# A first batch of 256 tokens taken tile by tile in a fused attention and FFN layer

## The reference

```
xn  = layernorm(x)
s   = attention(xn)            # Wqkv, 16 heads of 16, softmax(q k^T / 4) v, Wproj, bproj
g   = silu(gelu(xn W1^T + b1) W2^T + b2)      # 1024 hidden features
out = x + s * g
```

## Time and profile before

| | |
|---|---|
| time, three runs | 120.67, 120.86, 120.93 us |
| the profiled execution | 120.73 us |
| its span in the trace | 118.9 us |
| PE (TensorE) busy | 113.7 us (96% of the span) |
| VectorE, ScalarE, GpSimd busy | 84.8, 74.3, 70.3 us |
| TensorE at work without a break | from 7.63 us to 115.4 us |
| last store issued | 116.76 us |

### The profile page before, as it was taken

The page is one execution under the profiler, slowest core; times in us unless marked ns, Lnnn a source line. Parts: engine busy times, 40 slices in busy tenths (PEclk is TensorE's granted clock), DMA queues, the critical chain, the costliest instruction groups (busy, mean ns, idle before and its releaser), DMA issues.

```text
span 118.9 us, 2560 instructions
## 1 busy us (share of the span) xinstructions
PE 113.7 (96%) x930; PEld 88.4 (74%) x930; DVE 84.8 (71%) x159; ACT 74.3 (62%) x109; POOL 70.3 (59%) x91
## 2 busy tenths in 40 slices
PE   6989999999999999999999999999999999999980
PEld 5589998887878987888768777776775867566660
DVE  0799994520997989999899498205955848998762
ACT  4063795469979302231295979899868888799000
POOL 4227678009999904877889759589614341517460
PEclk9999999999999999999999999999999999999999
DMA  2999932666565366520000004500000000020213
GB/s 107 298 366 375 330 88 68 205 201 205 203 207 205 121 207 206 199 90 6 7 13 3 0 0 145 215 8 8 11 0 0 0 6 0 13 75 9 85 58 121
DMA packets 9632, 13.27 MB, mean 112 GB/s; under 512 B 2452, under 2 KB 4884, under 8 KB 9492
## 3 DMA queue, kind: packets, MB, share of 16 engines
q1 hardware_dynamic: 9332, 12.85, 32.5%
q10 hardware_dynamic: 288, 0.26, 0.7%
HBM read 5.51 MB, written 1.05 MB: 55 GB/s over the span
## 4 chain that ended last, share of the span: by engine, by line
PE 91%; DVE 2%; DMA 2%; issue 1%; POOL 1%; DVEq 0%; POOLq 0%
PE bank L794 39%; PE bank L903 14%; PE bank L920 12%; PE bank L884 9%; PE bank L870 8%; PE bank L900 6%; DMA xs<-x 2%; PE bank L827 2%; PE bank L931 1%; DVE fin L766 1%; DVE stats L608 1%; POOL rstd L392 1%; DVE fin L775 0%; PE bank L831 0%; DVE xs L623 0%
## 5 line engine op out<-in xcount | busy, mean ns | idle before, releaser
L687 DVE TENSOR_REDUCE negm<-bank 128x4 f32<-128x1024 f32 x32 | 37.3, 1216 | 9.8 <-PE bank L870 9.8
L451 POOL TENSOR_TENSOR hTl<-hG,hTh 128x512 fp32r<-128x512 f32 x16 | 20.4, 1295 | 8.7 <-ACT hTh L564 8.4
L903 PE MATMUL bank<-w2s,hTh 128*128 128x512 f32 x64 | 23.7, 410 | 0.0
L575 ACT ACTIVATE PT<-bank 128x1024 f32<-128x1024 f32 x16 | 15.4, 1027 | 2.8 <-PE bank L884 2.7
L900 PE MATMUL bank<-w2s,hTl 128*128 128x256 f32 x64 | 16.6, 280 | 0.0
L903 PEld LDWEIGHTS bank<-w2s,hTh 128*128 128x128 f32 x64 | 11.7, 188 | 3.1
L560 ACT ACTIVATE hG<-bank,b1s 128x512 f32<-128x512 f32 x16 | 10.9, 683 | 3.5 <-PE bank L794 3.4
L900 PEld LDWEIGHTS bank<-w2s,hTl 128*128 128x128 f32 x64 | 12.1, 188 | 0.5
L884 PEld LDWEIGHTS bank<-qs,ks 50*128 50x128 f32 x128 | 8.4, 185 | 3.8 <-issue 1.4
L884 PE MATMUL bank<-qs,ks 50*128 50x256 f32 x128 | 11.0, 299 | 0.0
L870 PEld LDWEIGHTS bank<-ks,qs 48*128 48x128 f32 x128 | 8.3, 185 | 3.3 <-issue 2.8
(11 more groups left out here) (94 smaller groups left out, 228.7 us busy)
## 6 DMA issues: line engine op xcount, KB each, us to landing
qs<-stage SPq DMA_DIRECT2D x24, 128.0 KB, 2.8
ks<-stage SPq DMA_DIRECT2D x24, 128.0 KB, 2.9
xs<-x SPq DMA_DIRECT2D x4, 256.0 KB, 3.9
w_raw<-w SPq DMA_DIRECT2D x1, 1024.0 KB, 7.5
w_in_place<-w SPq DMA_DIRECT2D x1, 1024.0 KB, 10.0
xb<-x SPq DMA_DIRECT2D x1, 1024.0 KB, 6.3
wqkv_raw<-wqkv SPq DMA_DIRECT2D x3, 256.0 KB, 4.6
out<-fin SPq DMA_DIRECT2D x6, 128.0 KB, 1.7
```

What stands on the lines that cost most here:

```text
L451: nc.gpsimd.tensor_tensor(hTl[:, n % FC, :], hG[:, n % FC, :], hTh[:, n % FC, :].bitcast(f32), ALU.subtract).then_inc(h_lo, 1)
L575: nc.scalar.activation(exp_of(w), scores_of(*s), ACT.Exp).then_inc(exp_done, 1)
L687: nc.vector.tensor_reduce(negm[:, j, :, s[1] % 2, b, :], scores_of(*s), axis=AX.X, op=ALU.max, negate=True).then_inc(max_done, 1)
L903: m = nc.tensor.matmul(bank_of("F2", u, 0), hTh[:, fc, c:c + P], w2s[:, fc].rearrange("p a e -> p (a e)"), start=fc == 0, stop=fc == FC - 1)
```

## The change

Six things change together.

1. `x` of the first batch comes in two DMAs of one tile each, then the weights of chunks 0 and 1, then `x` of batch 1, then the other weights as before.
2. The first batch is handled by tiles: statistics, epsilon, power, normalisation, two transposes (`XT0 t`), one copy (128x256) and one subtraction for each tile of 128 tokens. One `KEEP` instead of two.
3. The products of chunk 0 for the first 256 tokens are made by tile, 128 columns wide (`QT 0 a b t`). Those of chunks 1 to 3 stay 256 wide. For chunk 3 the pass (1, 0) is made once, 512 wide, at the end (`WIDE`). The rest of the list up to `QK 1` is put in another order.
4. The split of chunk 0's weights moves from VectorE to GpSimd; GpSimd splits the values' weights before the third batch's power; VectorE's statistics of batches 2 and 3 are spread; `V 0 1`'s copy and the second half of `w1h` follow `XT 3` on ScalarE.
5. The rows of ones are sent behind the whole restack.
6. GpSimd adds the residual of tile 6 too. For tile 7 VectorE writes its product back to PSUM and adds from there into `fin`.

The diff, cut to what the steps need:

```diff
@@ -20,7 +20,7 @@
-ON_POOL = (2, 3, 4, 5)
+ON_POOL = (2, 3, 4, 5, 6)
@@ -49,12 +51,13 @@
-    order = [("XT", 0)] + 2 * [("KEEP", 7)]
-    order += [("QA", i, a, b) for a, b in ((0, 0), (1, 0), (0, 1)) for i in (0, 1)]
-    order += [("QA", i, a, b) for a, b in ((0, 0), (0, 1)) for i in (2, 3)]
-    order += [("XT", 1)] + [("QA", i, 1, 0) for i in (2, 3)]
-    order += [("QK", 0, i) for i in CHUNKS]
-    order += [("XT", 2), ("V", 0, 0), ("XT", 3), ("V", 0, 1)] + [("QK", 1, i) for i in CHUNKS]
+    order = [("XT0", 0), ("KEEP", 7), ("XT0", 1)]
+    order += [("QT", 0, a, b, t) for t in range(2) for a, b in ((0, 0), (1, 0))]
+    order += [("QA", i, 0, 0) for i in (1, 2, 3)] + [("QT", 0, 0, 1, t) for t in range(2)]
+    order += [("QA", i, 0, 1) for i in (1, 2, 3)] + [("XT", 1), ("QA", 1, 1, 0), ("QK", 0, 0), ("QA", 2, 1, 0)]
+    order += [("QK", 0, i) for i in CHUNKS[1:]]
+    order += [("V", 0, 0), ("XT", 2), ("V", 0, 1), ("XT", 3)] + [("QK", 1, i) for i in CHUNKS]
@@ -323,10 +332,11 @@
-            for b in range(2):
-                sp.dma_start(xs[:, 2 * b:2 * b + 2, :], x_t[:, b, :]).then_inc(x_in[b], 16)
-            for c in range(2):
-                sp.dma_start(wqkv_raw[:, c], wqkv[c]).then_inc(wqkv_in[c], 16)
+            for t in range(2):
+                sp.dma_start(xs[:, t, :], x_t[:, 0, t * E:(t + 1) * E]).then_inc(x_first[t], 16)
+            sp.dma_start(wqkv_raw[:, 0], wqkv[0]).then_inc(wqkv_in[0], 16)
+            sp.dma_start(xs[:, 2:4, :], x_t[:, 1, :]).then_inc(x_in[1], 16)
+            sp.dma_start(wqkv_raw[:, 1], wqkv[1]).then_inc(wqkv_in[1], 16)
@@ -340,11 +350,6 @@
-            sp.wait_ge(ones_ready, 1)
-            for par in range(2):
-                sp.dma_start(ks[64 * par + STK:64 * par + STM, :, :].bitcast(f32)
-                             .rearrange("p h (b t) -> p (h b) t", t=SQ),
-                             ones[0:2, None, :].to_broadcast([2, HP * B, SQ])).then_inc(ones_rows, 16)
@@ -358,6 +363,12 @@
+            sp.wait_ge(ones_ready, 1)
+            for par in range(2):
+                sp.dma_start(ks[64 * par + STK:64 * par + STM, :, :].bitcast(f32)
+                             .rearrange("p h (b t) -> p (h b) t", t=SQ),
+                             ones[0:2, None, :].to_broadcast([2, HP * B, SQ])).then_inc(ones_rows, 16)
@@ -388,13 +399,21 @@
-                pool.wait_ge(veps_done, b + 1)
+                pool.wait_ge(veps_done, b + 2)
...
-            rsqrt(0)
+            for t in range(2):
+                pool.wait_ge(veps_done, t + 1)
+                nc.gpsimd.tensor_tensor(rstd[:, t:t + 1], veps[:, t:t + 1], mhalf[:, t:t + 1],
+                                        ALU.pow).then_inc(rstd_done, 1)
+            pool.wait_ge(xn_done, 2)
+            pool.wait_ge(wqk_hi, 1)
+            nc.gpsimd.tensor_tensor(quarter(wql, 0, 0), as_loaded(0, 0), quarter(wqh, 0, 0).bitcast(f32),
+                                    ALU.subtract).then_inc(wqk_lo, 1)
@@ -402,10 +421,9 @@
-            rsqrt(2)
-            pool.wait_ge(xn_done, 6)
...
+            rsqrt(2)
@@ -509,42 +527,56 @@
+            def high_w1(kc):
+                act.wait_ge(w1_in, 16)
+                nc.scalar.activation(w1h[:, kc, :], w1_raw[:, kc, :], ACT.Copy).then_inc(w1_hi, 1)
+            def take_v(h, p):
+                act.wait_ge(v_made, 2 * h + p + 1)
+                tt = 4 * h + 2 * p
+                nc.scalar.activation(VA[:, tt:tt + 2, :, 0:HN],
+                                     bank_of("V", h, p).rearrange("p (t n d) -> p t n d", t=2, d=HN),
+                                     ACT.Copy).then_inc(v_out, 1)
...
-            n_qk = n_v = n_f1 = late = 0
+            n_qk = n_f1 = late = 0
...
-                if s[0] == "XT":
+                if s[0] == "XT0":
+                    t = s[1]
+                    act.wait_ge(xt_made, t + 1)
+                    nc.scalar.activation(xTh[:, :, t * P:(t + 1) * P],
+                                         bank_of(*s)[:, 0:SQ].rearrange("p (k c) -> p k c", k=KC),
+                                         ACT.Copy).then_inc(xt_hi, 1)
+                    if t == 1:
+                        high_wqk(1)
+                        act.wait_ge(wqkv_in[2], 16)
+                        nc.scalar.activation(wqh[:, 2], wqkv_raw[:, 2], ACT.Copy).then_inc(wv_hi, 1)
+                elif s[0] == "XT":
...
-                    act.wait_ge(xt_made, b + 1)
+                    act.wait_ge(xt_made, b + 2)
...
-                    if b == 0:
-                        high_wqk(1)
-                        act.wait_ge(wqkv_in[2], 16)
-                        nc.scalar.activation(wqh[:, 2], wqkv_raw[:, 2], ACT.Copy).then_inc(wv_hi, 1)
+                    if b == 3:
+                        take_v(0, 1)
+                        high_w1(1)
...
-                    if n_qk in (2, 4):
-                        act.wait_ge(w1_in, 16)
-                        kc = n_qk // 2 - 1
-                        nc.scalar.activation(w1h[:, kc, :], w1_raw[:, kc, :], ACT.Copy).then_inc(w1_hi, 1)
+                    if n_qk == 1:
+                        high_w1(0)
...
-                    h, p = s[1:]
-                    act.wait_ge(v_made, n_v + 1)
-                    tt = 4 * h + 2 * p
-                    nc.scalar.activation(VA[:, tt:tt + 2, :, 0:HN],
-                                         bank_of(*s).rearrange("p (t n d) -> p t n d", t=2, d=HN),
-                                         ACT.Copy).then_inc(v_out, 1)
-                    n_v += 1
+                    if s != ("V", 0, 1):
+                        take_v(*s[1:])
...
-                        act.wait_ge(xt_made, B)
+                        act.wait_ge(xt_made, B + 1)
@@ -643,32 +684,41 @@
-            norm_stats(0)
-            norm_eps(0)
+            for t in range(2):
+                tile_stats(t)
+                tile_mean(t)
+                dve.wait_ge(mv_done, t + 1)
+                nc.vector.tensor_scalar_add(veps[:, t:t + 1], mv[:, t, 1:2], EPS).then_inc(veps_done, 1)
+            norm_apply(0)
...
-            norm_apply(0)
...
-            for q in range(2):
-                dve.wait_ge(wqk_hi, q + 1)
-                nc.vector.tensor_tensor(quarter(wql, 0, q), as_loaded(0, q), quarter(wqh, 0, q).bitcast(f32),
-                                        ALU.subtract).then_inc(wqk_lo, 1)
...
-                if s[0] == "XT":
+                if s[0] == "XT0":
+                    t = s[1]
+                    cols = slice(t * P, (t + 1) * P)
+                    dve.wait_ge(xt_hi, t + 1)
+                    nc.vector.tensor_tensor(xTl[:, :, cols], bank_of(*s)[:, 0:SQ].rearrange("p (k c) -> p k c", k=KC),
+                                            xTh[:, :, cols].bitcast(f32), ALU.subtract).then_inc(xt_lo, 1)
+                    if t == 1:
+                        norm_apply(1)
+                        dve.wait_ge(wqk_hi, 2)
+                        dve.wait_ge(wqk_lo, 1)
+                        nc.vector.tensor_tensor(quarter(wql, 0, 1), as_loaded(0, 1), quarter(wqh, 0, 1).bitcast(f32),
+                                                ALU.subtract).then_inc(wqk_lo, 1)
+                        tile_stats(4)
+                elif s[0] == "XT":
...
-                    if b == 0:
-                        norm_apply(1)
-                        norm_stats(2)
+                    if b == 1:
+                        tile_stats(5)
...
-                        norm_stats(3)
-                    if b == 1:
-                        norm_apply(2)
-                        norm_eps(3)
+                        tile_stats(6)
@@ -677,7 +727,10 @@
-                        norm_apply(3)
+                        tile_stats(7)
+                        norm_eps(3)
+                    if n_qk <= 2:
+                        norm_apply(n_qk + 1)
@@ -761,10 +814,11 @@
-                    if u >= 4:
+                    if 4 <= u < TT - 1:
...
-                    nc.vector.tensor_tensor(fin[:, u % 4, :], spot("PJ", u), gate[:, u, :],
-                                            ALU.mult).then_inc(gated, 1)
+                    nc.vector.tensor_tensor(fin[:, u % 4, :] if u < TT - 1 else spot("PJ", u), spot("PJ", u),
+                                            gate[:, u, :], ALU.mult).then_inc(gated, 1)
@@ -772,7 +826,10 @@
-                    nc.vector.tensor_tensor(fin[:, u % 4, :], fin[:, u % 4, :], xb[:, u, :], ALU.add).then_inc(fin_done, 1)
+                    if u == TT - 1:
+                        dve.wait_ge(stored[u - 4], 16)
+                    nc.vector.tensor_tensor(fin[:, u % 4, :], fin[:, u % 4, :] if u < TT - 1 else spot("PJ", u),
+                                            xb[:, u, :], ALU.add).then_inc(fin_done, 1)
@@ -818,7 +879,14 @@
-                if s[0] == "XT":
+                if s[0] == "XT0":
+                    t = s[1]
+                    pe.wait_ge(xn_done, t + 1)
+                    for kc in range(KC):
+                        last = nc.tensor.transpose(bank_of(*s)[:, kc * P:(kc + 1) * P],
```

(54 more changed lines are left out.)

1 line of the change is left out of this document (added).

## The result

The changed kernel takes 121.36 us, median of 11 runs (121.02 to 121.70); the kernel before, in as many runs beside it, 120.66 us (120.27 to 120.93). The ratio is 1.0059, 95% interval 1.0045 to 1.0073: slower by 0.7 us, as forecast (121.5, range 120.7 to 122.1; against the median of 120.86 that the forecast started from, 0.64 slower). The profiled execution took 121.52 us, with a span of 119.7; before, 120.73 and 118.9.

What follows compares the result with a forecast made beforehand. TensorE, busy 113.7 of 118.9 us, was taken as the bound, with front changes counted at the start of `QK 1 0`. Terms +1.0 - 0.12 - 0.2 = +0.7 gave 121.5 us, range 120.7 to 122.1.

Steps and rivals of the forecast that it cites:

- +1.0: Start of `QK 1 0`: 19.2 instead of 18.18 us, summed from -0.18, +0.46 and +0.73.
- The hold before `QK 1 0`: `XT 3` right in front of `QK 1 0`: TensorE idle, start 0.84 after the last transpose instead of 0.11, +0.73 us.
- Head start: Front of the kernel: first product at 6.87 us, 0.76 us earlier.
- Narrow products: First batch, chunk 0: 12 products 128 wide, 0.109 us apart, replace 6 that are 256 wide, +0.59 us.
- The rivals at 0.06 and 0.084: Narrow products' pace: 0.06 us apart gives 120.9 us, chance 0.12; 0.084 apart gives 121.2 us, chance 0.10.
- Hold at tile 1: First batch: tile 0's products end at 7.3, tile 1's wait until 7.6, plus 0.1 for what follows; +0.4 us.
- the upper end: Late tile 1: second power held by normalisation (+0.2), GpSimd's split late (+0.3), stores together (+0.2); 122.1 us, chance 0.11.
- Two 512-wide products: Chunk 3, before the values' step: two added products at 0.235 each, +0.46 us; values' step starts at 14.7.
- Weight splits: Splits of chunk 0, values and `w1h`: hidden; chunk 0's costs up to 0.3 us if the power is late.
- Rows of ones: Restack queue: ones sent behind it shorten the group of scores at 54.12 us from 1.03 to 0.91, -0.12 us.
- Tail: Tiles 6 and 7: tile 7's product starts 0.36 us earlier; bounds -0.36 and 0, taken as -0.2 us.
- The rival that ended faster: Narrow products cheap and the hold before `QK 1 0` gone or filled at once: 120.2 us, chance 0.12.

Runs made afterwards that it cites:

- experiment 8: Kernel before with only the tail changed: GpSimd adds tile 6's residual, tile 7 through PSUM, last projections in the tiles' order; 120.07 us, ratio 0.9956.
- experiment 1: Changed kernel with `XT 3` moved in front of `V 0 1`; 120.65 us, ratio 0.9998 to the kernel before.
- experiment 7: The best kernel: experiment 6 with both halves of tile 6's last projection in front of tile 7's; 119.31 us, ratio 0.9904 to the kernel before.
- experiment 4: Changed kernel with the rows of ones sent in front of the restack again; 121.61 us, ratio 1.0080 to the kernel before.
- experiment 6: Experiment 5 with `XT 1` also moved in front of the six products QA 1 to 3 (0, 1); 120.10 us, ratio 0.9962 to the kernel before.
- Experiment 3: Changed kernel with the old tail: VectorE adds the residual of tiles 6 and 7, both through `fin`; 121.52 us, ratio 1.0076 to the kernel before.
- experiment 5: Experiment 1 with ScalarE's copy of the values' weights moved behind the second batch's copies; 120.49 us, ratio 1.0000 to the kernel before.
- experiment 2: Changed kernel with chunk 0's products for the first batch 256 columns wide again; 121.37 us, ratio 1.0057 to the kernel before.
- experiment 9: Experiment 7 with the rows of ones in front of the restack again; 119.39 us, ratio 0.9905 to the kernel before.
- experiment 10: Experiment 7 with chunk 0's products for the first batch 256 columns wide; 119.26 us, ratio 0.9899 to the kernel before.
- experiment 11: Experiment 7 without the `KEEP` between the two tiles' transposes; 119.58 us, ratio 0.9922 to the kernel before.

## Why the prediction was right

The forecast was 0.7 us slower in the profile's terms, by +1.0, -0.12 and -0.2. The outcome was +0.75, nothing and nothing. The mechanism was right: the hold in front of `QK 1 0` was foreseen with its length, and it decides the result. That the total came out to within 0.1 us was luck: the sum had `QK 1 0` 0.25 too late (19.2, measured 18.93), and the two gains that it took off behind it, 0.32 together, weren't there.

- **Head start: right, partly for another reason.** First product at 6.81 (predicted 6.87). The tiles land at 3.01 and 3.34, one column's power takes 0.56 us and not the 0.72 of two columns, so the tiles are normalised by 5.0 and 5.7, and the warm-up products (to 5.8) and the lower clock set the start, as I had said.
- **Narrow products: right.** A stretch of four 128 wide and six 256 wide runs from 8.62 to 9.78; at 0.12 for each wide one that leaves 0.11 for a narrow one. The first ones' loads show it also. Timeline, kernel after:

```profile
6.78 0.30 PEld L851 LDWEIGHTS bank<-xTh,wqh 128*128 128x128 f32 x2 [0.20 <-issue]
6.81 0.41 PE L851 MATMUL bank<-xTh,wqh 128*128 128x128 f32 x2
...
7.38 0.41 PE L851 MATMUL bank<-xTh,wqh 128*128 128x128 f32 x2
...
8.62 1.32 PE L851 MATMUL bank<-xTl,wqh 128*128 128x128 f32 x10
```

  Weight loads (0.19 each, 0.30 for two) still start 0.11 apart. The Trainium skill (TensorE: Matmul & The Clock Gate, Back-to-back issue gap) gives 81 ns for a load and a product of 128 columns in a sustained stream; no stretch here reached it. The rivals at 0.06 and 0.084 are out.
- **Hold at tile 1: this step failed.** I had it at 0.4; it is 0.1. The distance of 0.84 was right: tile 1's last transpose starts at 6.54 (6.43 + 0.38 - 0.27) and its first product at 7.38. But that transpose came 0.18 before my 6.72, as the clock rose sooner here (6.40, in the kernel before 6.76). The 0.1 that I added for what follows wasn't at the hold, but the 20 products behind it took 2.40 us, 0.1 more than my pace gives. The second power was not late: GpSimd's two take 1.22 us together (4.02 to 5.24), so VectorE's epsilon and normalisation cost them nothing, and the contention that the Trainium skill (GPSIMD Engine Reference, Specifications) made me keep for the upper end doesn't show. So `XT 1` starts at 9.78, not 10.0, and against the profile before the front is worth -0.42, not -0.18. This is the quarter of a microsecond by which the +1.0 was too much between these two profiles. Against experiment 8's profile, which has the front of the kernel before, `XT 1` is only 0.07 sooner and `QK 1 0` 1.10 later. So single profiles give +0.75 or +1.10 for what I had at +1.0, and the size of this step's miss is not known to better than about 0.3 us.
- **Two 512-wide products: right,** +0.47: the values' step starts at 14.48, 3.54 us behind 10.94, where before it was 3.07 behind 11.36.
- **The hold before `QK 1 0`: right to 0.01 us** in length (0.84 from the last transpose), and experiment 1 shows that without it nothing of the slowdown is left: 0.71 by the medians. The rest of the front (-0.42) and the wide products (+0.47) cancel in the profiles.
- **Weight splits: hidden, as forecast,** in the kernel after: GpSimd's split of chunk 0 ends at 6.61, and the first product on it starts at 7.05. It isn't hidden in every execution. In experiment 7's profile, where TensorE comes sooner, the split ends at 6.55 and the first product on it starts at 6.70, 0.36 us behind the product in front of it; 0.11 would be the pace.
- **Rows of ones: this term failed,** though its row was read rightly. The group of scores at 55 us did shorten by 0.1, but experiment 4 has it as short with the ones in front, and experiment 8 with nothing of the kernel before changed ahead of it. I had taken a wait of one execution for a property of the kernel. The 0.1 is given back by 68 us besides, and I had not looked for whether it lasts.
- **Tail: this step failed.** VectorE's part did get 0.36 shorter, as worked out; but the two stores, issued 0.09 us apart, land 2.04 us after issue, not 1.70. I had taken -0.2 between the ends -0.36 and 0; the end 0 was right, for the reason that stood beside it. Experiments 7 and 8 show what was missing: the order of the projections, with which the tail is worth 0.32.

The rival that ended faster wanted the narrow products cheap and the hold gone. The hold goes with one line (experiment 1), and that alone brings the kernel level with before; experiment 6, with `XT 1` sooner, is ahead.

One reading of the prediction was wrong without harm: from 14.43 to 18.18 TensorE makes eight transposes and 24 products, not four and 24. With eight at 0.11 the products come 0.12 apart, which is the pace that the sum uses.

## What to carry to other kernels

When a list of steps is reordered, look for each place where a step stands directly behind the one whose result it needs by way of another engine: here it takes 0.84 us from the last transpose's start until a product can use it, so by my estimate, at 0.12 us a product, seven have to stand in between. Work that starts sooner is worth only what reaches the end of the chain; the early start at the front was spent on narrow products, on two wide ones and on a hole. A wait of 0.1 us, read from one profile, has to be seen in a second one before it is counted. At the end, have the tile before the last finished when the last one comes, and don't let the last two stores leave together.

## What the runs showed that I had not expected

- **The clock rises at another time in each execution.** Two `KEEP` products took 0.36 us at 6.24 in the kernel after, and 0.22 in the best kernel's profile, in which the first batch's transposes also came sooner. Chain of the best kernel:

```profile
5.64 0.22 PE bank L899 x2
...
6.24 0.38 PE bank L851 x2
```

  The work in front of it, ten warm-up products and two transposes, is the same in both. The upper level begins at 6.40 in the kernel after and at 4.22, still within the warm-up products, in the best kernel. By the records of the granted clock the upper level (2.4 GHz) begins between 4.2 us and 7.3 us from the span's start, over the eleven experiments' profiles; the lower one is 1.2 GHz. Experiments 6 and 7 have the same list at the front, and their first products start at 6.81 and 6.24: a single profile is no measure of a change of half a microsecond there. Experiment 3 has the front of the kernel after: there the upper level begins at 4.37 instead of 6.40, and `QK 1 0` starts at 18.39 instead of 18.93. It may also be the reason that medians and profiles disagree in experiments 4 and 5, which I haven't shown.
- **Two stores at once.** 128 KB each, issued 0.09 us apart: the last lands in 2.04 us (2.03 to 2.04 in the profiles of experiments 1, 2, 4, 5 and 6). Issued 0.5 us apart: 1.72 (1.72 in experiments 7 to 11).
- **The DMAs behind the rows of ones are issued more slowly.** SyncE's queue (timeline), first six restack DMAs of the kernel before, behind the ones, and of the kernel after, with nothing of the kind in front:

```profile
14.75 7.48 SPq L358 DMA_DIRECT2D qs<-stage  x6
```

```profile
13.52 3.85 SPq L363 DMA_DIRECT2D qs<-stage  x6
```

  The Trainium skill (DMA: Bandwidth & Descriptors, Why a DMA increments its semaphore by 16 and not by 1) says that the number of engines a DMA uses follows from its shape, so that one with a short outer dimension uses few. The rows of ones are such a DMA, but no trace here shows how many engines it used and no run varies its shape, so that the two partitions are the cause isn't shown. That the ones' place makes the difference is: in experiment 4, the kernel after with the ones in front, the six take 7.32 us. The 3.6 us cost nothing in this kernel (experiments 4 and 9), and so moving the ones brings nothing.
